# Row copies of the adjacency moved behind layer 0's attention, and operand halves made beside the first unit's masks

## What is computed

```python
# layer 0: attention, 4 heads of 64
ht = (h @ Wm).reshape(n, H, F)
scores = leaky_relu(el[:, :, None] + er.T[None, :, :], 0.2)
scores = where(adj[:, None, :] == 0, -inf, scores)
out = einsum('nhj,jhf->nhf', softmax(scores), ht)

# layer 1: a GRU on the edges, then three attention heads, then a second GRU
node_support = adj_norm @ h                      # adj_norm: adj without its diagonal
edge_output = gru_cell(node_support, h, ...)
hp = (adj_norm > 0) @ (h @ W)                    # per head
e_plus = leaky_relu([hp, hm] @ a)
att = softmax(where(adj_norm > 0, e_plus[None, :], NEG_INF))
edge_support += att * adj_norm @ (h @ W)
```

## Time and profile before

| what | value |
|---|---|
| median of 3 runs | 1327.91 us (1324.97 to 1328.03) |
| the profiled execution, its own time | 1326.06 us |
| its span | 1324.0 us |
| PE busy | 1139.3 us (86%) |
| DVE busy | 937.4 us (71%) |
| ACT busy | 784.3 us (59%) |
| POOL busy | 228.1 us (17%) |
| mean granted clock of PE | 0.94 |

### The profile page before, as it was taken

One profiled execution on the slowest core, in us unless ns is written; L12 is line 12 of the kernel. 1 busy time (PEld: TensorE's weight loads), 2 busy tenths in 40 slices (PEclk: granted clock), 3 DMA queues, 4 the chain that ended last, 5 costly groups with the idle time before them and its releaser, 6 DMA issues.

```text
span 1324.0 us, 35106 instructions
## 1 busy us (share of the span) xinstructions
PE 1139.3 (86%) x15054; PEld 937.7 (71%) x15054; DVE 937.4 (71%) x2037; ACT 784.3 (59%) x1001; POOL 228.1 (17%) x296
## 2 busy tenths in 40 slices
PE   4519898888866989999978999999999997778997
PEld 3418898888865766666656888888888654446886
DVE  5786677767995299999986998769995365553541
ACT  3479988778825123333327999989989365653000
POOL 5631011111103012222222000001220141220000
PEclk9759899999995889999989999999999998999999
DMA  9936567879518334433337345318852000020532
GB/s 217 179 52 68 63 73 115 117 108 133 71 3 293 101 100 124 116 114 111 106 111 223 106 143 197 114 59 294 286 186 104 5 29 17 16 96 1 189 118 87
DMA packets 128083, 153.77 MB, mean 116 GB/s; under 512 B 32065, under 2 KB 105393, under 8 KB 127665
## 3 DMA queue, kind: packets, MB, share of 16 engines
q1 hardware_dynamic: 74993, 127.05, 30.4%
q0 software_dynamic: 51744, 23.88, 15.8%
q10 hardware_dynamic: 1184, 0.53, 0.1%
HBM read 171.26 MB, written 35.60 MB: 156 GB/s over the span
## 4 chain that ended last, share of the span: by engine, by line
PE 54%; DVE 23%; issue 8%; ACT 6%; POOL 4%; DMA 3%; SPq 0%; DVEq 0%; POOLq 0%; ACTq 0%
PE PS L1620 18%; PE PS L1761 10%; PE PS L1762 9%; DVE scratch L1317 9%; PE PS L1815 8%; PE PS L1711 3%; POOL arena L704 2%; PE PS L1802 2%; DVE arena L1299 2%; DVE arena L1091 2%; PE PS L1718 1%; DVE arena L1343 1%; PE PS L1655 1%; DMA arena<-e_rows 1%; DMA arena<-in_edge_WhhT 1%
## 5 line engine op out<-in xcount | busy, mean ns | idle before, releaser
L1761 PE MATMUL PS<-arena 128*128 128x257 f16 x1452 | 325.3, 272 | 7.0 <-ACT arena L898 4.1
L1762 PE MATMUL PS<-arena 128*128 128x257 f16 x1452 | 325.3, 274 | 0.0
L1620 PE MATMUL PS<-arena 128*128 128x65 f16 x7744 | 260.1, 196 | 74.7 <-DVE arena L1137 40.4
L1620 PEld LDWEIGHTS PS<-arena 128*128 128x128 fp8e4 x7744 | 256.7, 99 | 78.0 <-issue 77.4
L812 ACT ACTIVATE arena<-arena 128x1408 fp8e4<-128x1408 f32 x176 | 241.9, 1456 | 45.9 <-DVE arena L1131 45.7
L1317 DVE CUSTOM_DVE_ANT_0 scratch<-arena 128x1408 bf16<-128x1408 bf16 x132 | 223.1, 1690 | 23.2 <-DMA arena<-e_rows 10.8
L898 ACT ACTIVATE arena<-arena 128x896 int16<-128x896 uint8 (+1 forms) x198 | 187.0, 971 | 22.1 <-DVE arena L1372 14.2
L1761 PEld LDWEIGHTS PS<-arena 128*128 128x128 bf16 x1452 | 142.7, 98 | 31.0 <-issue 8.2
L1762 PEld LDWEIGHTS PS<-arena 128*128 128x128 bf16 x1452 | 139.9, 96 | 21.5
L1131 DVE TENSOR_TENSOR arena<-arena,AT 128x352 int32<-128x352 int32 x176 | 91.2, 518 | 78.0 <-PE PS L1620 59.7
L889 ACT ACTIVATE arena<-arena,E1B 128x896 uint8<-128x896 f32 (+1 forms) x131 | 139.1, 1063 | 1.7 <-DMA arena<-m_rows 1.7
(11 more groups left out here) (189 smaller groups left out, 1338.3 us busy)
## 6 DMA issues: line engine op xcount, KB each, us to landing
arena<-adj_rows_half SPq DMA_DIRECT2D x88, 352.0 KB, 3.0
arena<-in_adj SPq DMA_DIRECT2D x44, 704.0 KB, 4.4
adj_rows_half<-in_adj POOLq DMA_DIRECT2D x22, 704.0 KB, 11.9
hw_saved<-arena SPq DMA_DIRECT2D x22, 387.0 KB, 4.2
AT<-in_adjT POOLq DMA_DIRECT2D x44, 176.0 KB, 8.3
arena<-hw_saved SPq DMA_DIRECT2D x9, 774.0 KB, 6.6
arena<-el_rows SPq DMA_DIRECT2D x8, 704.0 KB, 10.3
arena<-h_saved SPq DMA_DIRECT2D x44, 128.0 KB, 2.1
```

Of the source, the lines that this page charges most:

```text
L1620: ins = pe.matmul(PS[:, first_bank(n) + i, (2 * r + q) * C0:(2 * r + q + 1) * C0], MASK[:, (m + j) % NMASK, q, k * P:(k + 1) * P], MOV[:, ...
L1761: pe.matmul(PS[:, k, 0:D + 1], weights, w[:, 0:D + 1], start=(j == 0), stop=False)
L1762: ins = pe.matmul(PS[:, k, 0:D + 1], weights, w[:, D + 2:2 * D + 3], start=False, stop=(j == NT - 1))
```

## The change

- The operand halves are made inside the loop of unit 0. DVE makes products two tiles ahead, then in each step the next product, one low part and the masks; ACT makes the thresholds of three steps first (`AHEAD0 = 3`) and then one high half and one threshold in turn. PE takes the first four steps of unit 0 one by one, no longer together.
- DVE waits for the first half of the adjacency in two groups, 6 tiles and 16 tiles (`CHUNKS`).
- The row copies leave layer 0. Three are issued in the loop of norm and transposes (t = 12, 15, 18), one at t = 21 of it, one behind it, the others one per step of the edge stage, five tiles ahead (`ROWS_LEAD = 5`), with at most three in flight. A copy has 4 x 128 pieces of 704 elements, where it had 8 x 128 of 352.
- The diagonal is cleared tile by tile: a DMA of 128 single elements for each, issued by SP behind the loads of a step, and waited for ahead of the next step's loads.

```diff
+    AHEAD0 = 3
+    CHUNKS = [(0, 6), (6, 22)]
+    ROWS_LEAD = 5
@@ sync
-            sp.wait_ge(sem("rows_h"), 16 * NT)
-            sp.dma_start(AH_D.rearrange("t p n -> (t p n)")[0:(P - 1) * NT * (N + 1)]
-                         .rearrange("(a b c) -> a b c", b=NT, c=N + 1)[:, :, 0:1],
-                         ZB[0:P - 1, :].unsqueeze(2), allow_slow_non_contiguous=True).then_inc(sem("rows_z"), 16)
-            sp.wait_ge(sem("rows_z"), 16)
...
+            def clear_diagonal(t):
+                n = P if t < NT - 1 else P - 1
+                sp.wait_ge(*row_copied(t))
+                sp.dma_start(AH_D.rearrange("t p n -> (t p n)")[t * P * (N + 1):(t * P + n) * (N + 1)]
+                             .rearrange("(a c) -> a c", c=N + 1)[:, 0:1],
+                             ZB[0:n, 0:1], allow_slow_non_contiguous=True).then_inc(sem("rows_z"), 16)
...
+            for t in range(ROWS_LEAD - 1):
+                clear_diagonal(t)
+            sp.wait_ge(sem("rows_z"), 16 * (ROWS_LEAD - 1))
             for L in range(2):
                 load_row(L)
...
             for t in range(NT):
                 if t + 2 < NT:
                     load_h(t + 2, HR, 0)
+                if 1 <= t and t + ROWS_LEAD - 2 < NT:
+                    sp.wait_ge(sem("rows_z"), 16 * (t + ROWS_LEAD - 1))
                 for L in range(loads_before(t + 1) if t else 2, loads_before(t + 2)):
                     load_row(L)
+                if t + ROWS_LEAD - 1 < NT:
+                    clear_diagonal(t + ROWS_LEAD - 1)
@@ gpsimd
-            for t in range(NT):
-                pool.wait_ge(sem("masks_built"), 68 + 4 * t)
-                pool.dma_start(AH_D[t].rearrange("p (c n) -> c p n", c=8), ...).then_inc(sem("rows_h"), 16)
...
+            def copy_row(t):
+                if t >= 3:
+                    pool.wait_ge(*row_copied(t - 3))
+                pool.dma_start(AH_D[t].rearrange("p (c n) -> c p n", c=4), ...).then_inc(row_copied(t)[0], 16)
...
             for t in range(NT):
                 pool.wait_ge(sem("h1"), t + 1)
                 pool.tensor_copy(HHL[:, t, 0, :], H32R[:, t % 8, :]).then_inc(sem("hi1"), 1)
+                if t >= 12 and t % 3 == 0:
+                    copy_row(t // 3 - 4)
+            copy_row(ROWS_LEAD - 1)
...
             for t in range(NT + 1):
+                if t + ROWS_LEAD < NT:
+                    copy_row(t + ROWS_LEAD)
                 if t < NT:
                     delta(t, 0, HR, GT)
@@ scalar
-            act.wait_ge(sem("mov"), NT)
+            weighted_high(0)
+            weighted_high(1)
             act.wait_ge(sem("u_mm"), 1)
+            act.wait_ge(sem("elb0"), 16)
+            for j in range(AHEAD0):
+                threshold(0, j)
             for n, (g, h) in enumerate(units0):
                 act.wait_ge(sem(f"elb{n % 2}"), 16 * (n // 2 + 1))
                 for j in range(NT):
-                    threshold(n, j)
+                    if n == 0 and j + 2 < NT:
+                        weighted_high(j + 2)
+                    if n > 0:
+                        threshold(n, j)
+                    elif j + AHEAD0 < NT:
+                        threshold(0, j + AHEAD0)
@@ vector
+            weighted(0)
+            weighted(1)
             for m in range(last + 1):
                 n, j = divmod(m, NT)
+                if m + 2 < NT:
+                    weighted(m + 2)
+                if m < NT:
+                    low_part(m)
                 positive_mask(m)
@@ tensor
-                for js in rounds(4):
+                for js in (rounds(4) if n > 0 else [[j] for j in range(4)] + rounds(4)[1:]):
```

More of the change, by code:

```diff
@@ L158, in gnn_stack_kernel @@
         RD = a0.take(11)
-        ZB = a0.take(NT, dt=BF16, size=2)
         NOTB = a0.take(P, dt=FP8, size=1)
@@ L168, in gnn_stack_kernel @@
         HTF = AT[:, :, htf_at:htf_at + 4 * H0 * C0].bitcast(F32)
-        assert NREAL <= (P - 1) * NT
         THRi = THR.bitcast(mybir.dt.int32)
@@ L265, in gnn_stack_kernel @@
         DN = sb("DN", [P, NT])
-        NOTI = sb("NOTI", [P, P])
+        NOTI = sb("NOTI", [P, P], BF16)
+        ZB = sb("ZB", [P, 2], BF16)
         identh = sb("identh", [P, P], F16)
@@ L366, in gnn_stack_kernel, with row_copied @@
         assert max(row_at) < CHECK_FIRST - 2
+        copy_sems = [("adj_a0", CHUNKS[0][1]), ("adj_a1", NT - CHUNKS[0][1]), ("adj_b", NT)]
+        def row_copied(t):
+            name, before = copy_sems[t % 3]
+            return sem(name), 16 * (before + t // 3 + 1)
         def half_of(L):
@@ L540, in _ @@
                     load_h(t + 2, HR, 0)
+                if 1 <= t and t + ROWS_LEAD - 2 < NT:
+                    sp.wait_ge(sem("rows_z"), 16 * (t + ROWS_LEAD - 1))
                 for L in range(loads_before(t + 1) if t else 2, loads_before(t + 2)):
+                    assert half_of(L)[0] <= t + ROWS_LEAD - 2 or t + ROWS_LEAD - 2 >= NT - 1
                     load_row(L)
+                if t + ROWS_LEAD - 1 < NT:
+                    clear_diagonal(t + ROWS_LEAD - 1)
                 if t == NT - 2:
@@ L654, in _ @@
             pool.memset(ALR, 0.0).then_inc(sem("consts"), 1)
-            link(pool.memset(ZB, 0.0))
+            link(pool.memset(ZB[:], 0.0))
             pool.memset(ET[:], 1.0).then_inc(sem("consts"), 1)
@@ L665, in _ @@
             for t in range(NT):
-                pool.dma_start(AT[:, t, 0:GA[0][1] * P], adjT[t, :, 0:GA[0][1] * P]).then_inc(sem("adj_a"), 16)
+                part = [i for i, (t0, t1) in enumerate(CHUNKS) if t0 <= t < t1][0]
+                pool.dma_start(AT[:, t, 0:GA[0][1] * P], adjT[t, :, 0:GA[0][1] * P]).then_inc(sem(f"adj_a{part}"), 16)
             for i in range(len(pieces)):
@@ L686, in _ @@
                 pool.dma_start(AT[:, t, GA[0][1] * P:NT * P], adjT[t, :, GA[0][1] * P:NT * P]).then_inc(sem("adj_b"), 16)
-            for t in range(NT):
-                pool.wait_ge(sem("masks_built"), 68 + 4 * t)
-                pool.dma_start(AH_D[t].rearrange("p (c n) -> c p n", c=8),
-                               t_in["adj"][t * P:(t + 1) * P, :].rearrange("p (c n) -> c p n", c=8)).then_inc(sem("rows_h"), 16)
             pool.wait_ge(sem("dn"), 16)
@@ L695, in _ @@
             pool.memset(UP[:, :, 3 * H1:3 * H1 + 1], 1.0).then_inc(sem("consts"), 1)
+            def copy_row(t):
+                if t >= 3:
+                    pool.wait_ge(*row_copied(t - 3))
+                pool.dma_start(AH_D[t].rearrange("p (c n) -> c p n", c=4),
+                               t_in["adj"][t * P:(t + 1) * P, :].rearrange("p (c n) -> c p n", c=4)
+                               ).then_inc(row_copied(t)[0], 16)
             for t in range(NT):
@@ L799, in _, with weighted_high @@
             act.wait_ge(sem("coef"), 1)
-            for t in range(NT):
+            def weighted_high(t):
                 act.wait_ge(sem("t_b"), t + 1)
@@ L1092, in low_part, with weighted @@
                                   MOV[:, t, :, 0, :], ALU.subtract).then_inc(sem("mov"), 1)
-            for t in range(NT):
+            def weighted(t):
                 if t >= 3:
@@ L1100, in _ @@
                                   ALU.mult).then_inc(sem("t_b"), 1)
-                if t >= 1:
-                    low_part(t - 1)
-            low_part(NT - 1)
             def mask_words(m, q):
@@ L1118, in positive_mask @@
                 dve.wait_ge(sem("t_act"), m + 1)
-                if h == 0 and j == 0:
-                    dve.wait_ge(sem(["adj_a", "adj_b"][g]), 16 * NT)
+                for part, (t0, t1) in enumerate(CHUNKS):
+                    if m == t0:
+                        dve.wait_ge(sem(f"adj_a{part}"), 16 * (t1 - t0))
+                if g == 1 and h == 0 and j == 0:
+                    dve.wait_ge(sem("adj_b"), 16 * NT)
                 if m == 0:
```

## The result

| | before | changed |
|---|---|---|
| median of 4 runs | 1326.44 us | 1343.9 us |
| span of the profiled execution | 1324.0 us | 1342.3 us |
| layer 0's last matmul ends | 387.25 | 362.89 |
| L1655 / L1701 (484 matmuls) starts | 422.38 | 400.60 |
| second row maximum starts | 464.42 | 458.09 |

The ratio is 1.014, 95% interval 1.0106 to 1.0173: the changed kernel is slower, by 17 us, where the prediction had it 14 us faster. The table says where: 24.4 us ahead at the end of layer 0, 6.3 us ahead when the row maxima begin, 17.5 us behind when they end. Behind the edge stage 0.8 us more is lost.

A forecast was written before the change was run, and what follows sets the result against it. PE was taken to bound layer 0, PE and DVE level in the edge stage. Terms -3 + 1 - 21 + 2 + 3 + 4 = -14 gave 1312, against the median 1314 us; range for 8 in 10 1297 to 1333.

The forecast's parts named there:

- start and burst: Layer 0's start: operand halves in unit 0's loop, -3 us; POOL's second group of adjacency loads in a burst, +1 us.
- copies out of layer 0: Layer 0 from 189 to 363 us: PE's gaps beside row copies alone go, 26.6 us falling to 5.2; -21 us.
- (a): Loop of norm and transposes: POOL issues three copies between casts, partly within its wait for ACT; +2 us.
- (b): The 484 short matmuls behind layer 0: copies in flight make PE's instruction fetch late; +3 us.
- (c): Ahead of the edge stage: h_turned store and row loads wait for four clears, but copies are in by 440; 0 us.
- (e): Edge loop: one copy a step makes the DMA share 0.87, still under 1; +4 us together with (f).
- (f): Edge loop: row loads wait behind clears on SP, 0.2 us a step over 20 steps; +4 us, bounds 0 and 31.
- its own sign of being wrong: Edge stage: the prediction is wrong if DVE's L1317 waits over 1 us a step for row loads.
- rival 2: Edge stage: row loads come late behind the clears, costing 31 us in place of 4; 1341 us, chance 0.14.
- rival 3: Layer 0: PE's gaps don't come from the copies, so the start gives 3 and moves cost 10; 1335 us, chance 0.05.

The follow-up runs named there:

- e14: The changed kernel with each row copy in 2 x 128 pieces of 1408 elements in place of 4 x 128; 1446.03 us in its one run.
- e1: The changed kernel with row copies in 8 x 128 pieces of 352 elements in place of 4 x 128; 1318.27 us, ratio 0.9912 to the kernel before.
- e2: The changed kernel with row copies in 16 x 128 pieces of 176 elements in place of 4 x 128; 1313.96 us, ratio 0.9869 to the kernel before.
- e11: The changed kernel with each copy written rows outermost, going out as 32 pieces of 11264 elements; 1318.34 us, ratio 0.9887 to the kernel before.
- e4: The changed kernel without the clears of the diagonal, SP waiting for the landed copies instead; 1340.27 us, ratio 1.0057 to the kernel before.
- e8: The changed kernel with SP's first four clears, their wait and two row loads behind the h_turned and e_rows stores and e_rows loads; 1346.25 us, ratio 1.0115.

## Why the prediction was wrong, step by step

| term | predicted | measured | where |
|---|---|---|---|
| units 0 and 1: start and burst | -3, +1 | +2.6 | unit 0 -2.0, unit 1 +4.6 |
| copies out of layer 0 | -21 | -26.9 | units 2 to 7: 219.7 to 192.7 |
| (a) loop of transposes | +2 | +2.6 | 35.1 to 37.7 |
| (b) 484 matmuls | +3 | +0.7 | gaps of 2.00 and 1.05 for 2.31 |
| (c) up to the row maxima | 0 | +14.7 | chain above |
| (e), (f) edge stage | +4 | +23.8 | 226.2 to 250.0 |
| sum | -14 | +18.3 | with 0.8 behind the stage |

(c) is what is left between the rows above it and the second row maximum, -6.3.

**The step that failed** is the one on the pieces: the prediction took 4 x 128 for 8 x 128 as fewer pieces and hence a cheaper issue, and used "up to 11.9 us to landing" and "5.4 us of all 16 engines" for the new copy. Both were measured on copies with eight outermost rows. With four, the same engine time is on four engines and the landing is 21.6 us. The runs e14, e1 and e2 change this number alone, with 2, 8 and 16, and e11 gives 32 by turning the dimensions round; the landing follows it, and so do the edge stage and the time up to 16. A cheaper issue did not come either: the issue took 1.15 us, where it was 1.06.

**Term (c)** failed by the same landing, counted twice. Its two times, "in by 440" and the e_rows store at 449.77, are both in the clock of the kernel before, so both move ahead with layer 0, and 10 us lay between them. But the fourth copy waits for the first. Two landings came to 40.5 us, where twice 11.9 is 23.8. That used up the 10 us and 6.4 more, and sent h_turned out beside the store. The bound of 5.4 us had no place for either. With landings of 13.1 or 9.5 us (e1, e2) the chain at this place is as predicted: the store leaves at 426.77 and 430.66 and nothing holds it.

**Term (f)** had named the place: row loads late behind SP's waits, and from 1.55 us a step it costs 31. Measured were 32.2 us of waits for row loads in the stage, 1.6 a step, over the 1 us that the prediction set as its own sign of being wrong. The term was given 0.2 us a step on the ground that a copy is in flight for less than half of a step. One was in flight all of the time: 21.6 us of landing against steps of 10 to 17 us. That ground failed on the prediction's own rows as well, since 11.9 us is longer than its step of 11. With the landing it assumed (e1, 13.1) the stage costs 9.6 us more than before, not 4. The average share, 0.69 measured and 0.87 predicted, gave no warning; the four engines under the copy decided, not the sixteen. Only with 16 pieces does the stage cost 4.2 us more than before, the +4 of the prediction. So rival 2 was nearly right on the time (1341) and on the place, but its cause, the clears, is worth 3.7 of the 23.8 us in the stage (e4).

**The terms of layer 0** held in sum, -24.4 for -23, by luck: two errors cancel. The copies' move was worth 26.9 and not 21; what is left in gaps after 189 us, 5.23 us, is what the prediction left (5.2). The other 5.6 us are not in the gaps: the same matmuls ran in less time, at a granted clock of 0.99 where it was 0.97; behind the two longest gaps of before, 128 of them took 5.66 and 5.69 us for 4.22, at a granted clock of 0.72. The start gave 2.0 for 3, and DVE's step was 2.25 us as predicted, though by other parts: 0.34, 0.61, 0.44 and 0.86, the extra having moved from the low part to the mask. Unit 1 took 4.6 us more for the +1 of the burst, near its bound of 5. The reading of the gaps as late fetches is shown by the q8 block that lands just before each ends; that q0 holds them up is borne out by their going with its traffic, and rival 3 falls. q0 is not all of it: the 1.90 us before 291.62 end with such a block too, but stand where from 288 to 292 us q0 moves nothing and q1 carries a load of elb.

## What to carry to other kernels

Before a copy is re-cut, look at the outermost number of its pattern and not at the length or the count of its pieces: below 16 it narrows the copy to so many engines, and everything beside it that is spread over all 16 waits for the busy ones, at any average share. When a wait has two landings in a row behind it, its margin shrinks by twice the error in the landing. And work that is taken away from the head of a unit is gone only if what it releases (here the second adjacency group) has somewhere quiet to land; here unit 1 gave back what unit 0 had won.

## What the hardware did that was not expected

- Narrow copies slow what lies beside them more than their bytes say: from 500 to 640 us row loads landed in a median of 6.5 us and stores of products in 9.5 us beside copies on four engines, and in 4.6 and 3.9 us beside copies on 16, at a higher DMA share of the stage (0.82 for 0.69).
- In the chains shown a clear of 128 single elements took 5.05 to 5.95 us beside copies; one of 2794 took 34.62 us.
- PE's waits at multiples of 128 matmuls end 1.2 to 1.6 us after a block of 16384 bytes on q8 has landed, in all 31 cases of layer 0 after 125 us in the two kernels.
- SP's own issue of two e_rows loads took from 3.17 us (e2) to 10.40 us (e8).
- POOL and DVE disturb each other by pairs of instructions: the same product of POOL cost DVE 0.42 us whether it ran beside the low part or beside a mask.
